# Two graph layers on one core: residual slots of their own, the next x transposed a step later, and three GpSimd and ScalarE tasks moved

## The reference, cut to what matters

```
e0 = leaky(einsum('bid,bjd->bij', h * a0[:, 0], h))          # one kind of edge occurs: adj == 1
x  = layernorm(x + einsum('bij,bjd->bid', sigmoid(where(adj == 1, e0, -big)), h) + bias)
Hh = x @ W;  e = where(adj != 0, exp(-leaky(s[:, None] + d[None, :])), 0)
x  = layernorm(x + elu((e @ Hh) / rowsum(e)))
```

## Time and profile before

| | |
|---|---|
| median of three runs | 1384.6 us (1381.48 to 1385.0) |
| the profiled execution, its own time | 1382.85 us |
| its span, first to last instruction | 1381.2 us |
| TensorE busy | 1286.2 us, 93% of the span |
| VectorE, ScalarE, GpSimd busy | 1012.6, 859.5, 839.0 us |
| mean granted TensorE clock | 0.984 of full speed |

### The profile page before, as it was taken

One profiled execution on the slowest core, in us unless ns is written; L12 is line 12 of the kernel. 1 busy time (PEld: TensorE's weight loads), 2 busy tenths in 40 slices (PEclk: granted clock), 3 DMA queues, 4 the chain that ended last, 5 costly groups with the idle time before them and its releaser, 6 DMA issues.

```text
span 1381.2 us, 27397 instructions
## 1 busy us (share of the span) xinstructions
PE 1286.2 (93%) x7874; PEld 1152.9 (83%) x7874; DVE 1012.6 (73%) x2594; ACT 859.5 (62%) x2129; POOL 839.0 (61%) x1228
## 2 busy tenths in 40 slices
PE   4799999999999999999999999999999999999996
PEld 3688888988888898888888888898888888888885
DVE  3777778777777777778777787777768777787765
ACT  3666757567574765757567584765747566574743
POOL 4565838567393765838557394765838557394732
PEclk9999999999999999999999999999999999999999
DMA  6353251623406144251623406144251623506101
GB/s 145 58 85 93 47 106 39 106 72 65 106 20 117 61 77 98 40 102 48 106 72 60 111 16 121 61 73 97 42 99 53 106 72 55 114 17 116 36 1 33
DMA packets 190353, 101.73 MB, mean 74 GB/s; under 512 B 140657, under 2 KB 173809, under 8 KB 190321
## 3 DMA queue, kind: packets, MB, share of 16 engines
q1 hardware_dynamic: 171888, 67.79, 20.8%
q0 software_dynamic: 18432, 33.56, 14.4%
HBM read 84.55 MB, written 16.78 MB: 73 GB/s over the span
## 4 chain that ended last, share of the span: by engine, by line
PE 44%; POOL 23%; DVE 18%; issue 7%; ACT 6%; DMA 1%; DVEq 1%; POOLq 0%; SPq 0%; ACTq 0%
POOL coef_lo L368 12%; PE acc_bank L1209 9%; PE hh_bank L1188 6%; PE acc_bank L1090 5%; PE acc_bank L1091 5%; PE acc_bank L1092 5%; DVE coef L867 5%; PE lg_bank L1090 3%; POOL rstd L389 3%; PE lg_bank L1092 3%; PE lg_bank L1091 3%; DVE stats L909 2%; DVE resid L904 2%; PE xt_bank L1163 2%; DVE score L763 2%
## 5 line engine op out<-in xcount | busy, mean ns | idle before, releaser
L1209 PE MATMUL acc_bank<-H,coef 128*128 128x258 f32 x2048 | 467.5, 381 | 10.7 <-ACT reluP L605 9.4
L1209 PEld LDWEIGHTS acc_bank<-H,coef 128*128 128x128 f32 x2048 | 380.3, 189 | 73.4 <-issue 20.1
L368 POOL TENSOR_TENSOR coef_lo<-coef,coef_hi 128x1024 fp32r<-128x1024 f32 x128 | 306.1, 2392 | 68.6 <-ACT coef_hi L553 68.1
L1090 PE MATMUL acc_bank<-h_hi,coef_hi 128*128 128x256 f32 x1024 | 303.6, 296 | 1.8 <-issue 1.8
L1091 PE MATMUL acc_bank<-h_lo,coef_hi 128*128 128x256 f32 x1024 | 292.1, 285 | 0.0
L1092 PE MATMUL acc_bank<-h_hi,coef_lo 128*128 128x256 f32 x1024 | 291.7, 285 | 0.0
L867 DVE SCALAR_TENSOR_TENSOR coef<-tr_bank,E_col,codeT 128x256 f32<-128x256 f32 x512 | 209.2, 476 | 38.2 <-PE acc_bank L1209 35.7
L1090 PEld LDWEIGHTS acc_bank<-h_hi,coef_hi 128*128 128x128 f32 x1024 | 200.6, 196 | 2.6 <-issue 2.0
L1091 PEld LDWEIGHTS acc_bank<-h_lo,coef_hi 128*128 128x128 f32 x1024 | 200.6, 196 | 0.0
L1092 PEld LDWEIGHTS acc_bank<-h_hi,coef_lo 128*128 128x128 f32 x1024 | 200.2, 196 | 0.0
L553 ACT ACTIVATE coef_hi<-coef 128x1024 fp32r<-128x1024 f32 x128 | 135.7, 1061 | 88.5 <-DVE coef L804 86.9
(11 more groups left out here) (76 smaller groups left out, 2282.0 us busy)
## 6 DMA issues: line engine op xcount, KB each, us to landing
code_nat<-in_adj POOLq DMA_DIRECT2D x128, 256.0 KB, 4.2
x_raw<-in_x SPq DMA_DIRECT2D x16, 1024.0 KB, 5.7
out<-x SPq DMA_DIRECT2D x128, 128.0 KB, 1.7
codeT<-code_nat SPq DMA_TRANSPOSE x128, 3.3
W_ext<-in_L_gnn_W SPq DMA_DIRECT2D x1, 256.0 KB, 2.8
score<-in_L_gnn_a SPq DMA_DIRECT2D x1, 256.0 KB, 6.1
bias_bc<-in_L_gnn_bias SPq DMA_DIRECT2D x1, 128.0 KB, 3.7
a_col<-in_L_gnn_a SPq DMA_DIRECT2D x4, 1.0 KB, 2.2
```

Of the source, the lines that this page charges most:

```text
L368: nc.gpsimd.tensor_tensor(coef_lo[:, t % 4, :, :], blocks(coef[:, t % 4, :]), f32(coef_hi[:, t % 4, :, :]), ALU.subtract).then_inc(S.lo0, 1)
L1090: nc.tensor.matmul(dst, lhs_hi, rhs_hi, start=first, stop=False)
L1209: ins = nc.tensor.matmul(acc_bank[t % 2][:, 0:HC], coef[:, SLOT1[t], J * P:(J + 1) * P], H[:, J, :], start=J == 0, stop=J == NT - 1)
```

## The change

Five edits, in one diff:

- Layer 1 gets slots 2 and 3 of `stats`, `moments`, `var_eps` and `rstd`, and keeps its residual in `reluP` in place of `resid`. `residual0` loses its wait for `norm1`; `elu_parts` gains a wait for the `norm1` two tiles before, since that now reads `reluP`.
- `XT_STEP` moves the four quarters of the next x from steps 2 to 5 to steps 3 to 6. Chunks 0 and 1 move from steps 5 and 6 to steps 6 and 7 on TensorE, their scaling and leaky part from 6 and 7 to 7 and 8, and those of chunk 2 behind step 8. On VectorE `low_xT` of the last two quarters, steps 5 and 6, stands ahead of `norm0`; in the version before this held for the last one.
- `next_bias`, one tile a step from step 2 on, becomes two tiles a step from step 5 on, ahead of `power0`.
- `power1` and `norm1` of tile 7 of the graph before move from step 1 to step 5.
- `watch_codes` is done for tiles 0 to 3 at steps 0 to 3 and for tiles 4 to 7 at steps 5 to 8 (it was tiles 0 to 5 at steps 0 to 5, and 6 and 7 at 6 and 7). `low0` at step t waits for `norm0` of tile t-1.

```diff
-    XT_STEP = {2: 0, 3: 1, 4: 2, 5: 3}
+    XT_STEP = {3: 0, 4: 1, 5: 2, 6: 3}
@@ GpSimd, power1: moments, var_eps and rstd at 2 + t % 2
@@ GpSimd, graph
                 for t in range(NT + 1):
+                    if nxt and t >= 5:
+                        if t == 5:
+                            pool.wait_ge(F.x_loaded, 16 * (b + 2))
+                        next_bias(b, 2 * t - 10)
+                        if t < NT:
+                            next_bias(b, 2 * t - 9)
                     if t >= 1:
                         power0(F, b, t - 1)
-                    if prev and t == 1:
+                    if prev and t == 5:
                         power1(F, b - 1, NT - 1)
-                    if nxt and t >= 2:
-                        if t == 2:
-                            pool.wait_ge(F.x_loaded, 16 * (b + 2))
-                        next_bias(b, t - 2)
                     if 1 <= t and t + 3 < NT:
+                        pool.wait_ge(F.x1, NT * b + t)
                         low0(F, b, t + 3)
@@ ScalarE, elu_parts
+                if t >= 2 or S is F and (not isinstance(b, int) or b > 0):
+                    act.wait_ge(S.y, NT * b + t - 1)
                 nc.scalar.activation(reluP[:, t % 2, :], acc_bank[t % 2][:, 0:D], ACT.Relu,
@@ ScalarE, graph
-                    if t < 6:
+                    if t < 4:
                         watch_codes(b, t)
                     if 1 <= t and t + 3 < NT:
                         high0(F, b, t + 3, prev)
-                    if t == 1 and prev:
+                    if t == 5 and prev:
                         norm1(F, b - 1, NT - 1)
-                    if nxt and 6 <= t:
-                        scale_scores(b + 1, t - 6)
-                    if t in (6, 7):
-                        watch_codes(b, t)
+                    if nxt and 7 <= t:
+                        scale_scores(b + 1, t - 7)
+                    if t >= 5:
+                        watch_codes(b, t - 1)
+
+                if nxt:
+                    scale_scores(b + 1, 2)
                 keep_H(F, b, 6, prev, False)
@@ VectorE, residual0
                 if t >= 2:
                     dve.wait_ge(S.x1, NT * b + t - 1)
-                elif prev:
-                    dve.wait_ge(S.y, NT * b + t - 1)
@@ VectorE, residual1: the second operation writes reluP, not resid
-                if t >= 2:
+                if t >= 2 or prev:
                     dve.wait_ge(S.y, NT * b + t - 1)
-                else:
-                    dve.wait_ge(S.x1, NT * b + t + 7)
@@ VectorE, graph
-                    if nxt and t == 5:
+                    if nxt and 5 <= t and t in XT_STEP:
                         low_xT(F, b + 1, XT_STEP[t], False)
                     if t >= 1:
                         norm0(F, b, t - 1, prev)
@@
-                    if nxt and 6 <= t:
-                        leaky_scores(b + 1, t - 6)
+                    if nxt and 7 <= t:
+                        leaky_scores(b + 1, t - 7)
+                if nxt:
+                    leaky_scores(b + 1, 2)
                     leaky_scores(b + 1, 3)
@@ TensorE, graph
-                    if nxt and 5 <= t < 7:
-                        if t == 5:
+                    if nxt and 6 <= t:
+                        if t == 6:
                             pe.wait_ge(F.xT_lo, 4 * (b + 1) + 3)
                         else:
                             pe.wait_ge(F.xT_lo, 4 * (b + 1) + 4)
-                        scores_chunk(b + 1, t - 5)
+                        scores_chunk(b + 1, t - 6)
```

More of the change, by code:

```diff
@@ L195, in two_graph_layers @@
         resid = sb("resid", [P, 2, D])
[L196 to L199, removed]
+        stats = sb("stats", [P, 4, 6])
+        moments = sb("moments", [P, 4, 2])
+        var_eps = sb("var_eps", [P, 4, 1])
+        rstd = sb("rstd", [P, 4, 1])
         neg_mean = sb("neg_mean", [P, 2, 1])
@@ L384, in power1 @@
                 pool.wait_ge(S.moments1, NT * b + t + 1)
-                nc.gpsimd.tensor_tensor(neg_mean[:, t % 2, :], zero_col[:, :], moments[:, t % 2, 0:1], ALU.subtract)
-                nc.gpsimd.tensor_tensor(var_eps[:, t % 2, :], moments[:, t % 2, 1:2], eps_col[:, :],
+                nc.gpsimd.tensor_tensor(neg_mean[:, t % 2, :], zero_col[:, :], moments[:, 2 + t % 2, 0:1], ALU.subtract)
+                nc.gpsimd.tensor_tensor(var_eps[:, 2 + t % 2, :], moments[:, 2 + t % 2, 1:2], eps_col[:, :],
                                         ALU.add).then_inc(S.var1, 1)
                 pool.wait_ge(S.var1, NT * b + t + 1)
-                nc.gpsimd.tensor_tensor(rstd[:, t % 2, :], var_eps[:, t % 2, :], neg_half[:, :],
+                nc.gpsimd.tensor_tensor(rstd[:, 2 + t % 2, :], var_eps[:, 2 + t % 2, :], neg_half[:, :],
                                         ALU.pow).then_inc(S.rstd1, 1)
                 pool.wait_ge(S.rstd1, NT * b + t + 1)
-                nc.gpsimd.tensor_tensor(shift[:, t % 2, :], neg_mean[:, t % 2, :], rstd[:, t % 2, :],
+                nc.gpsimd.tensor_tensor(shift[:, t % 2, :], neg_mean[:, t % 2, :], rstd[:, 2 + t % 2, :],
                                         ALU.mult).then_inc(S.shift1, 1)
@@ L610, in norm1 @@
                 act.wait_ge(S.shift1, NT * b + t + 1)
-                nc.scalar.activation(x1[:, t, :], resid[:, t % 2, :], ACT.Identity, bias=shift[:, t % 2, :],
-                                     scale=rstd[:, t % 2, :]).then_inc(S.y, 1)
+                nc.scalar.activation(x1[:, t, :], reluP[:, t % 2, :], ACT.Identity, bias=shift[:, t % 2, :],
+                                     scale=rstd[:, 2 + t % 2, :]).then_inc(S.y, 1)
             def graph(b, prev, nxt):
@@ L807, in mask0_rest, with residual0 @@
                 ins.then_inc(F.mask0, 1)
-            def residual0(S, b, t, prev):
+            def residual0(S, b, t):
                 if t >= 2:
                     dve.wait_ge(S.x1, NT * b + t - 1)
-                elif prev:
-                    dve.wait_ge(S.y, NT * b + t - 1)
                 dve.wait_ge(S.agg0, NT * b + t + 1)
@@ L891, in row_inverse, with residual1 @@
                 nc.vector.reciprocal(rinv[:, t % 2, :], rowsum[:, t % 2, :]).then_inc(S.rinv, 1)
-            def residual1(S, b, t):
-                if t >= 2:
+            def residual1(S, b, t, prev):
+                if t >= 2 or prev:
                     dve.wait_ge(S.y, NT * b + t - 1)
-                else:
-                    dve.wait_ge(S.x1, NT * b + t + 7)
                 dve.wait_ge(S.relu, NT * b + t + 1)
@@ L903, in residual1 @@
                 dve.wait_ge(S.elu, NT * b + t + 1)
-                nc.vector.scalar_tensor_tensor(resid[:, t % 2, :], reluP[:, t % 2, :], -1.0, x1[:, t, :],
+                nc.vector.scalar_tensor_tensor(reluP[:, t % 2, :], reluP[:, t % 2, :], -1.0, x1[:, t, :],
                                                ALU.add, ALU.add).then_inc(S.resid1, 1)
@@ L908, in stats1 @@
                 dve.wait_ge(S.resid1, NT * b + t + 1)
-                nc.vector.bn_stats(stats[:, t % 2, :], resid[:, t % 2, :]).then_inc(S.stats1, 1)
+                nc.vector.bn_stats(stats[:, 2 + t % 2, :], reluP[:, t % 2, :]).then_inc(S.stats1, 1)
             def moments1(S, b, t):
@@ L913, in moments1 @@
                 dve.sem_inc(dve_past, 1)
-                nc.vector.bn_aggr(moments[:, t % 2, :], stats[:, t % 2, :]).then_inc(S.moments1, 1)
+                nc.vector.bn_aggr(moments[:, 2 + t % 2, :], stats[:, 2 + t % 2, :]).then_inc(S.moments1, 1)
             def graph(b, prev, nxt):
@@ L919, in graph @@
                     if t >= 1:
-                        residual0(F, b, t - 1, prev)
+                        residual0(F, b, t - 1)
                     if 1 <= t < 3:
@@ L972, in graph @@
                     if t >= 1:
-                        residual1(F, b, t - 1)
+                        residual1(F, b, t - 1, prev)
                         stats1(F, b, t - 1)
@@ L1063, in _ @@
                                     dve.wait_ge(GEN.summed, 2 * (NT * b + t) + k)
-                        residual0(GEN, b, t, False)
+                        residual0(GEN, b, t)
                         stats0(GEN, b, t)
@@ L1079, in _ @@
                         row_inverse(GEN, b, t, False)
-                        residual1(GEN, b, t)
+                        residual1(GEN, b, t, False)
                         stats1(GEN, b, t)
```

## The result

The changed kernel takes 1463.84 us (median of 4 runs, 1460.69 to 1465.2), the one before 1383.62 in the same comparison: a ratio of 1.058, 95% interval 1.0567 to 1.0593. That is 80 us slower, where 28 were forecast, and above the forecast's range and every rival in it. The direction and the places were right; the size was not.

What follows compares the result with a forecast made beforehand. TensorE, busy for 93% of the span, was taken as the bound. 0.7 + 0.8 + 0.75 = 2.25 us on 82.82 gives 85.07 against 83.06; 2.0 times 14 is 28 us, 1382.85 + 28 = 1411 us, range 1374 to 1424.

Steps and rivals of the forecast that it cites:

- every rival in it: Loose knot, 1373 to 1363 (chance 0.16); ScalarE's stall mostly hidden, 1380 to 1398 (0.17); clock drops too, 1420 to 1430 (0.1).
- Tile 1: TensorE's layer 0 wait for `norm0` of tile 1 shrinks from 2.06 to 1.6 us, with no clock drops counted.
- The first graph's 3.72 us: Time from `low0` to `norm0` of tile 1 in the first graph, taken as model for the middle graphs.
- The reading of the drops: Ten of thirteen TensorE waits of 1.98 us and more precede a drop to 1.2 GHz; one of 1.71 does not.
- Tiles 2 to 4: `norm0` of tiles 2 and 3 comes just in time for TensorE; at tile 4 TensorE waits 0.8 us.
- ScalarE at step 5: ScalarE stands still 3.8 us before `norm1` of tile 7; TensorE then waits 0.5 at `project` of tile 4, 1.4 at tile 5.
- The transposes a step later: Chunk 1 after tile 7's sum adds 0.8 us; chunk 3 waits 0.75 for `leaky_scores` of chunk 1.
- the quarter of 0.5 that was still owed: A quarter of the next x no longer lies ahead of tile 2 on TensorE; 0.5 us to be done later.
- The mask: `mask0_rest` on VectorE should get longer, with `low0` moved onto it; 2.24 us under `low0` in the first graph.
- "then 0.41 and 0.15": At step 5, after late `low_xT`: 0.41 us for `norm0` of tile 5 and 0.15 to TensorE.
- the path to chunk 3's scores: `leaky_scores` of chunk 1 behind two stages of mask and `norm0`: 3.8 us after tile 7's sum, against chunk 3's 3.06.
- The drop was a rival: The clock also drops at the step 5 waits, half of 3.4 us in ten graphs; 1420 to 1430 us, chance 0.1.

Runs made afterwards that it cites:

- adj_late: The changed kernel with the eight adjacency loads in one block behind step 8, none in steps 5 to 8; 1411.15 us, ratio 1.0206.
- bias_late: The changed kernel with the eight bias sums in one block behind step 8, loads left straight behind `power0`; 1392.18 us, ratio 1.0058.
- slots_late: The kernel before with layer 1's own slots and the later transposes and chunks, all else as before; 1395.62 us, ratio 1.0073.
- slots_only: The kernel before with layer 1's own slots alone; 1376.63 us, ratio 0.9952.
- both_back: The changed kernel with bias sums back at steps 2 to 8 and `power1` and `norm1` of tile 7 back at step 1; 1397.7 us, ratio 1.0116.
- adj_late_tail: The changed kernel with adjacency loads behind step 8 and `power1` and `norm1` of tile 7 back at step 1; 1396.73 us, ratio 1.0082.
- tail_back: The changed kernel with `power1` and `norm1` of tile 7 back at step 1; 1430.82 us, ratio 1.035.
- loads_first: The kernel before with only its adjacency loads moved ahead of the bias sum in steps 5 to 8; 1397.05 us, ratio 1.0097.
- best_bl: The kernel before with layer 1's own slots, `power1` and `norm1` of tile 7 at step 6, eight bias sums behind step 8; 1365.95 us, ratio 0.9866.

## Why the prediction was wrong in size

**Tile 1: right.** The wait is 1.54 us over the middle graphs for a forecast of 1.6, and no drop of the clock follows it in the changed kernel. The first graph's 3.72 us was a good model, contention included: 3.69 here (587.28 to 590.97). The reading of the drops was looser than it looked. The kernel before has fourteen waits of 1.98 us and more, not thirteen, and ten have a drop. And waits of 1.5 to 1.6 us are no safeguard: in adj_late two of the fourteen at tile 1 (1.54 and 1.60 us) are followed by a drop, in bias_late three. That none came here is in part luck.

**Tiles 2 to 4: right.** 0 to 0.24 us at tiles 2 and 3, 0.62 at tile 4 for 0.8.

**ScalarE at step 5: right in size, overpriced a little.** 3.77 us for 3.8. Its price was 1.6 us a graph at most, where the two waits that the forecast hung on it make 1.9 (0.5 and 1.4); `project` of tile 4 waited 0.14 us where the forecast had 0.5.

**The transposes a step later: right.** 0.75 us for chunk 3 plus the quarter of 0.5 that was still owed, against 1.30. The expectation of slots_late counted the 0.75 alone and missed.

**The mask.** `mask0_rest` got longer, as forecast, but the new wait of `low0` is hardly the reason: of the 186 ns that its mean gained, 138 are there in slots_only, which does not have that wait.

**The step that failed** is "then 0.41 and 0.15", the cost of `norm0` of tile 5, and the same 0.41 unspoken in the path to chunk 3's scores. The forecast had used the two lengths of `norm0` (0.41 alone, 0.81 under a bias sum) at tile 1 and did not ask which applied at tiles 5 to 7, where it had just put two sums a step ahead of `power0` and so left the loads and the next step's sums directly behind it. The term was 0.41 three times; it measured 1.19, 1.35 and 1.42. From 85.01 (adj_late) to 88.63 that is 3.6 us a graph, in three shares: tile 5's wait 0.9 longer, the chunk waits 1.3 longer (2.35 for 1.06), and one drop of the clock in each of the 14 middle graphs, at 1.5 us each, where adj_late has two in all. The drop was a rival, at about the right price (1.7 us) but with a chance of 0.1, because the forecast's waits stayed under the 1.98 us after which drops had been seen; the wait of 2.1 us at tile 5 does not.

**Loads and sums 3.6, ScalarE's wait 1.1, the transposes 1.3, less 0.4 for own slots** is 5.6 us, the whole of 88.63 less 83.07. The spread code checks and `low0`'s wait add 0.08 (both_back less slots_late), and the sums two a step with the loads behind step 8 take off 0.17 (adj_late_tail against both_back). These are the shares in this order of steps; as the pieces do not add up, another order gives others.

**What stays open** is how a bias sum that has not begun can hold `norm0`. In the middle graphs of the changed kernel, tail_back and loads_first it is stretched wherever it begins in the issue of the second load and the sum directly behind begins at most 0.53 us later. In five cases of tail_back, in the same order, the sum begins 0.54 to 0.58 us later, and `norm0` takes 0.41 us. At tile 7 of bias_late and best_bl GpSimd has a wait of its own between the loads and the sum, and `norm0` takes 0.41 us in all 28 cases; but there too the sum begins 0.53 to 0.55 us later. The distance alone could explain all of them, and no run tells it from the wait. Nor does a run show whether the coming sum already claims something that `norm0` needs, or whether it begins earlier than the profile, which is rough on GpSimd, records.

## What to carry to other kernels

When work is moved on one engine, read what it will then lie beside on the others: the same instructions in another order on GpSimd cost 67 us here, most of it through VectorE (3.6 of 4.7 us a graph, by adj_late) and the rest through ScalarE. Price an instruction by the row in which its neighbours are the ones it will have, and where the trace has two lengths for it, decide at each place which one holds. And a move that frees one wait is worth only what the next one leaves: the transposes were taken out of a stretch in which TensorE waited anyway.

## What the runs showed of the hardware that was not expected

- A `norm0` of 128 x 256 floats takes 0.41 us alone, 0.81 when a GpSimd sum of the same shape starts just before it, and then ends 0.15 us after the sum. With two sums, or with loads and then sums, it takes 1.25 to 2.12 us, and again ends 0.16 us after the last sum. That looks less like time shared than like an instruction held until GpSimd is through. The Trainium skill (GPSIMD Engine Reference, Key points) says that GpSimd contends with VectorE instructions that have two SBUF inputs or run in a two-port mode. The trace agrees that there is contention, 0.41 us becoming 0.81, though it does not show in which mode `norm0` runs; the runs add that `norm0` is held to the end of the queued sums.
- GpSimd's issue of a DMA, 0.55 us of its time, does not hold the same instruction up at all: 0.40 to 0.41 us under it in bias_late, tiles 6 and 7, 28 cases.
- In six graphs TensorE waits 2.1 us and, 8.6 us after that, 2.3 to 2.4 us; the granted clock drops once, behind the second. In the eight others it drops behind the first, and the second wait is 1.6 to 1.7 us. The length of a wait did not decide alone: drops followed waits of 1.5 to 1.6 us in adj_late and bias_late, and four of 2.06 to 2.16 us in the kernel before were followed by none.
